# Expert stage of a cross-attention and mixture-of-experts kernel: seven masked tiles, three-wide elementwise operations, no GpSimd work

## The reference, cut to what matters

```python
top_p, top_i = jax.lax.top_k(probs, K)                      # K = 2 of E = 8
for _ in range(NUM_ITER):                                   # 2
    ctx = jnp.concatenate([integrated, v], axis=-1)
    shared_ctrl = _gelu(ctx @ w_s1 + b_s1) @ w_s2 + b_s2
    x_shared, v_shared = _inl(shared_ctrl, integrated, v, mu)
    hidden = _gelu(jnp.einsum('tc,tch->th', ctx_e, w1) + b1)   # w1, b1 of the token's two experts
    ctrl = jnp.einsum('th,tho->to', hidden, w2) + b2
    x_r, v_r = _inl(ctrl, x_e, v_e, mu)
    x_r = (x_r * flat_w).reshape(B * N, K, Dm).sum(axis=1)
    v_r = (v_r * flat_w).reshape(B * N, K, Dm).sum(axis=1)
    x_next = sw * x_shared + (1.0 - sw) * x_r
    v_next = sw * v_shared + (1.0 - sw) * v_r
    halt = jax.nn.sigmoid(_gelu(x_next @ w_h1 + b_h1) @ w_h2 + b_h2)
    refined = _gelu(x_next @ w_f1 + b_f1) @ w_f2 + b_f2
    integrated = integrated + halt * refined * integration_weight
    v = v_next
```

## Time and profile before

| what | us |
|---|---|
| runs (3): median, lowest, highest | 426.99, 422.50, 427.07 |
| profiled execution, first to last instruction (span) | 421.0 |
| PE, DVE, ACT, POOL busy in it | 382.0, 330.7, 203.8, 79.4 |

### The profile page before, as it was taken

One profiled execution on the slowest core, in us unless ns is written; L12 is line 12 of the kernel. 1 busy time (PEld: TensorE's weight loads), 2 busy tenths in 40 slices (PEclk: granted clock), 3 DMA queues, 4 the chain that ended last, 5 costly groups with the idle time before them and its releaser, 6 DMA issues.

```text
span 421.0 us, 4354 instructions
## 1 busy us (share of the span) xinstructions
PE 382.0 (91%) x1394; PEld 220.2 (52%) x1394; DVE 330.7 (79%) x744; ACT 203.8 (48%) x295; POOL 79.4 (19%) x62
## 2 busy tenths in 40 slices
PE   4999997899968799799999899999999999999774
PEld 4746963545635355365545535646464573647521
DVE  0748757655775899897999997997899699799593
ACT  2401135665655725726558256364644635463922
POOL 0210011000010002032231340361015007201500
PEclk9989999999998969889899899999999999979978
DMA  8999320000000000000000000000000000000001
GB/s 275 427 359 303 136 75 1 2 0 0 2 1 0 2 0 1 2 0 1 0 0 2 1 0 0 2 0 0 2 1 0 0 2 26 0 2 1 25 0 51
DMA packets 10727, 17.87 MB, mean 42 GB/s; under 512 B 336, under 2 KB 8528, under 8 KB 9552
## 3 DMA queue, kind: packets, MB, share of 16 engines
q1 hardware_dynamic: 10704, 17.59, 12.1%
HBM read 16.54 MB, written 1.05 MB: 42 GB/s over the span
## 4 chain that ended last, share of the span: by engine, by line
PE 54%; DVE 26%; ACT 8%; issue 7%; POOL 2%; DMA 1%; POOLq 0%; SPq 0%; DVEq 0%; ACTq 0%
PE bank L1010 51%; DVE ring L794 4%; DVE zz L709 3%; DVE hm_lo L803 2%; DVE hm_hi L799 2%; POOL lrs L290 2%; DVE lst L694 2%; DMA ctxT<-in_ctxT 1%; DVE b L968 1%; ACT vtok L534 1%; ACT L534 1%; PE bank L1093 1%; DVE b L976 1%; ACT L483 1%; DVE kT L991 1%
## 5 line engine op out<-in xcount | busy, mean ns | idle before, releaser
L794 DVE SCALAR_TENSOR_TENSOR ring<-ring,pB 128x512 f32<-128x512 f32 x64 | 59.0, 961 | 18.3 <-issue 10.1
L1010 PE MATMUL bank<-hm_hi,ew_hi 128*128 128x512 f32 x160 | 71.6, 447 | 0.0
L1010 PE MATMUL bank<-hm_hi,ew_lo 128*128 128x512 f32 x160 | 64.8, 405 | 0.0
L1010 PE MATMUL bank<-hm_lo,ew_hi 128*128 128x512 f32 x160 | 64.6, 404 | 0.0
L1010 PE MATMUL bank<-xi,pB 128*128 128x512 f32 (+2 forms) x88 | 45.6, 621 | 2.5 <-ACT xi L357 0.7
L803 DVE TENSOR_TENSOR hm_lo<-ring,hm_hi 128x512 fp32r<-128x512 f32 x64 | 41.0, 679 | 0.0
L1010 PEld LDWEIGHTS bank<-hm_hi,ew_hi 128*128 128x128 f32 x160 | 32.3, 202 | 7.4 <-issue 1.3
L1010 PEld LDWEIGHTS bank<-hm_hi,ew_lo 128*128 128x128 f32 x160 | 31.9, 199 | 6.8
L1010 PEld LDWEIGHTS bank<-hm_lo,ew_hi 128*128 128x128 f32 x160 | 31.5, 197 | 7.2
L426 ACT ACTIVATE ring<-bank,pB 128x512 f32<-128x512 f32 x32 | 21.9, 688 | 21.4 <-PE bank L1010 21.4
L290 POOL TENSOR_TENSOR lrs<-lve,mhalf 128x4 f32<-128x4 f32 x12 | 12.1, 1007 | 105.9 <-DVE lve L699 105.9
(11 more groups left out here) (215 smaller groups left out, 667.8 us busy)
## 6 DMA issues: line engine op xcount, KB each, us to landing
ring<-in_fc1b SPq DMA_DIRECT2D x4, 1024.0 KB, 17.3
ring<-in_fc2a SPq DMA_DIRECT2D x4, 1024.0 KB, 9.2
...
a<-in_fc1a SPq DMA_DIRECT2D x1, 1024.0 KB, 13.1
...
```

The source lines that it names most:

```text
L794: dve.scalar_tensor_tensor(hm[j % 2], idxb[:, c, k, :], W("tile_expert", j, j + 1), hid[:, j, :], ALU.is_equal, ALU.mult).then_inc(sem("hm ...
L1010: return pe.matmul(out, lhsT, rhs, start=start, stop=stop)
```

## The change

The expert stage is written anew. The two slots of a token are now sorted by expert number (the smaller first), and the expert tiles are stored in the order 0, 7, 1 to 6. Expert 0 can only be in the first slot and expert 7 only in the second, so that tile 0 serves both slots at once and there are 7 masked tiles. The control networks of shared, first and second slot write three neighbouring banks (`group_ps`), and all activations and most DVE operations take the three streams as one operand of 1536 columns. Tile 0 and its bias are multiplied as halves of 64 rows. The shared hidden units stand twice on the partitions and are cut into fp32r parts as well (`shared_halves`). GpSimd's share goes to DVE. `refine` runs one step later, `bias_parts` moves to slot 1 after the load of one pack `in_C` (1344 KB in place of 768 KB), and `route` and `weigh` are written with compares and reductions over 4 x 8 values, each waiting for the one before (`link`): 15 operations in place of 15, and 8 in place of 5. The index tile is bf16.

The core of the diff (removed lines stand above, apart from those of GpSimd):

```diff
+ORDER = (0, 7, 1, 2, 3, 4, 5, 6)
+TILES = ((0, None), (1, 0), (1, 1), (2, 0), (2, 1), (3, 0), (3, 1))
+NT = len(TILES)
...
+            sp.dma_start(ring[:, PC0:PC0 + nC], d_packC).then_inc(sem("in_C"), 16)
...
-            def refined(s):
-                c = s % NCH
-                pool.wait_ge(sem("rr"), 2 * s + 2)
-                pool.tensor_tensor(xi[:, ck(c)], xi[:, ck(c)], rr, ALU.add).then_inc(sem("xi"), 1)
-                if s >= NCH:
-                    pool.wait_ge(sem("xi"), s + 1)
-                    pool.tensor_tensor(res[:, ck(c)], xi[:, ck(c)], xT[:, ck(c)], ALU.add)\
-                        .then_inc(sem("res"), 1)
-            for s in range(STEPS):
-                c = s % NCH
...
-                for k in range(2):
-                    pool.tensor_tensor(ew[:, 2 + k, :], ew[:, 0, :], cb[:, c, k, :], ALU.mult)\
-                        .then_inc(sem("ew"), 1)
...
+            def squashed(s, part):
+                n = group_of(s, part)
+                act.wait_ge(sem("part_ps"), n + 1)
+                if s >= 1:
                     act.wait_ge(sem("xn"), s)
...
+                if part == BETA:
+                    act.activation(bg[:, 0], group_ps(n), ACT.Abs).then_inc(sem("ab"), 1)
+                    act.wait_ge(sem("ab"), 2 * s + 1)
+                    act.activation(bg[:, 0], bg[:, 0], ACT.Tanh, scale=0.5).then_inc(sem("ab"), 1)
+                    act.wait_ge(sem("ab"), 2 * s + 2)
+                    act.activation(bg[:, 0], bg[:, 0], ACT.Ln, bias=half_col[:, 0:1], scale=0.5)\
+                        .then_inc(sem("squash"), 1)
+                else:
+                    out = al if part == ALPHA else bg[:, 1]
+                    act.activation(out, group_ps(n), ACT.Tanh, scale=0.5).then_inc(sem("squash"), 1)
...
             for s in range(STEPS):
...
                 if s + 1 < STEPS:
                     hidden_gelus(s + 1)
...
+                if s >= 2:
+                    refine2(s - 2)
+                if s < NCH:
+                    squashed(s, GATE)
+                    if s == 0:
+                        expand_evac(NCH - 1, 7, 6)
+                    squashed(s, BETA)
+                    if s >= 1:
+                        refine1(s - 1)
                 else:
...
+                    squashed(s, ALPHA)
+                    squashed(s, GATE)
                     refine1(s - 1)
...
+                    squashed(s, BETA)
+            refine2(STEPS - 2)
             refine1(STEPS - 1)
             refine2(STEPS - 1)
...
+                    bias_parts()
...
+                    hidden_masked(0, (0,))
+                    hidden_masked(0, (1, 2))
                 if q:
                     route(t - 2)
                 if f:
                     ln_scale("att", t)
...
+            hidden_masked(0, (3, 4))
             weigh(NCH - 1)
...
+            hidden_masked(0, (5, 6))
+            shared_halves(0)
+            dve.wait_ge(sem("consts"), 2)
+            def stepped(s):
+                c, it2 = s % NCH, s >= NCH
+                x, v = xi[:, ck(c)], vT[:, ck(c)]
+                def thrice(a):
+                    return a.unsqueeze(1).to_broadcast([128, 3, CH])
+                if it2:
+                    dve.wait_ge(sem("squash"), group_of(s, ALPHA) + 1)
+                    link(dve.scalar_tensor_tensor(al, al, 1.0, thrice(v), ALU.add, ALU.mult))
+                link(dve.tensor_scalar(ne, x, W("mu"), -1.0, ALU.subtract, ALU.mult))
+                dve.wait_ge(sem("squash"), group_of(s, GATE) + 1)
+                dve.wait_ge(sem("squash"), group_of(s, BETA) + 1)
+                dve.scalar_tensor_tensor(bg[:, 0], group_ps(group_of(s, BETA)), 0.0, bg[:, 0],
+                                         ALU.max, ALU.subtract).then_inc(sem("sp"), 1)
...
+                if it2:
+                    link(dve.tensor_tensor(bg[:, 0], bg[:, 0], thrice(ne), ALU.mult))
+                    link(dve.scalar_tensor_tensor(al, al, 0.5, bg[:, 0], ALU.mult, ALU.add))
+                    link(dve.scalar_tensor_tensor(bg[:, 1], bg[:, 1], 1.0, al, ALU.add, ALU.mult))
+                    link(dve.tensor_tensor(bg[:, 1, 1:3], bg[:, 1, 1:3], cb[:, c], ALU.mult))
+                    both = bg[:, 1]
+                    link(dve.scalar_tensor_tensor(both[:, 0], both[:, 0], swc[:, 2:3], both[:, 1],
+                                                  ALU.mult, ALU.add))
+                    link(dve.tensor_tensor(both[:, 0], both[:, 0], both[:, 2], ALU.add))
+                else:
+                    link(dve.tensor_tensor(bg[:, 0, 1:3], bg[:, 0, 1:3], cb[:, c], ALU.mult))
+                    link(dve.scalar_tensor_tensor(bg[:, 1], bg[:, 1], 1.0, bg[:, 0], ALU.add, ALU.mult))
+                    link(dve.scalar_tensor_tensor(bg[:, :, 0], bg[:, :, 0], swc[:, 2:3], bg[:, :, 1],
+                                                  ALU.mult, ALU.add))
+                    link(dve.tensor_tensor(bg[:, :, 0], bg[:, :, 0], bg[:, :, 2], ALU.add))
+                    dve.tensor_tensor(v, bg[:, 0, 0], ne, ALU.mult).then_inc(sem("v1"), 1)
+                    link(dve.tensor_tensor(bg[:, 1, 0], bg[:, 1, 0], ne, ALU.mult))
+                if s >= 1:
+                    dve.wait_ge(sem("h1_ps"), s)
+                dve.scalar_tensor_tensor(xn, bg[:, 1, 0], 0.05, x, ALU.mult, ALU.add).then_inc(sem("xn"), 1)
...
             for s in range(STEPS):
...
                 if s >= 1:
...
+                    stepped(s - 1)
+                if s >= 2:
+                    refine(s - 2)
...
+                    for tiles in ((0,), (1, 2), (3, 4), (5, 6)):
+                        hidden_masked(s + 1, tiles)
+                    shared_halves(s + 1)
+                if s == 0:
+                    slot_masks(NCH - 1)
+                    slot_weights(NCH - 1, 7, 6)
+            stepped(STEPS - 1)
+            refine(STEPS - 2)
             refine(STEPS - 1)
...
+            def controls(s, part):
...
+                n = group_of(s, part)
+                o = slice(part * D, (part + 1) * D)
+                sh, lo, hi = (bank[3 * (n % 2) + k] for k in range(3))
+                top, bot = slice(0, 64), slice(64, 128)
+                m = masked(s)
+                h = hsh[:, s % 2, :]
...
+                if n >= 2:
+                    r, was = owner(n - 2)
+                    if was == BETA:
+                        pe.wait_ge(sem("sp"), r + 1)
+                    else:
+                        pe.wait_ge(sem("squash"), n - 1)
+                pe.wait_ge(sem("m72"), c + 1)
+                pe.wait_ge(sem("hsl"), s + 1)
+                pe.wait_ge(sem("hlo"), NT * s + 1)
+                w_hi, w_lo = weights(ew2_hi, 0), weights(ew2_lo, 0)
+                mm(lo, bp_e[top, o], m72[top, ck(c)], stop=False)
+                mm(hi, bp_e[bot, o], m72[bot, ck(c)], stop=False)
+                mm(lo, w_hi[top, :], m[top, 0, 0, :], start=False, stop=False)
+                mm(hi, w_hi[bot, :], m[bot, 0, 0, :], start=False, stop=False)
+                mm(lo, w_lo[top, :], m[top, 0, 0, :], start=False, stop=False)
+                mm(hi, w_lo[bot, :], m[bot, 0, 0, :], start=False, stop=False)
+                mm(lo, w_hi[top, :], m[top, 1, 0, :], start=False, stop=False)
+                mm(hi, w_hi[bot, :], m[bot, 1, 0, :], start=False, stop=False)
+                mm(sh, ws2_lo[top, o], h[top, :], stop=False)
+                mm(sh, bp_s[top, o], onesb[top, :], start=False, stop=False)
+                mm(sh, ws2_hi[:, o], h, start=False)
+                for i in range(1, NT):
+                    j, k = TILES[i]
+                    pe.wait_ge(sem("hlo"), NT * s + i + 1)
+                    out = hi if k else lo
+                    mm(out, weights(ew2_hi, j), m[:, 0, i, :], start=False, stop=False)
+                    mm(out, weights(ew2_lo, j), m[:, 0, i, :], start=False, stop=False)
+                    last = mm(out, weights(ew2_hi, j), m[:, 1, i, :], start=False, stop=j == HT - 1)
+                last.then_inc(sem("part_ps"), 1)
...
+                pe.wait_ge(sem("h1"), s + 1)
+                if s + 3 < STEPS:
+                    pe.wait_ge(sem("hid"), HT * (s + 4))
+                    pe.wait_ge(sem("hs"), s + 4)
...
                 if s + 1 < STEPS:
                     hidden(s + 1)
...
+                if s >= 2:
+                    refine_b(s - 2)
+                if s < NCH:
+                    controls(s, GATE)
+                    if s == 0:
+                        pe.wait_ge(sem("hid"), 2 * HT)
+                        pe.wait_ge(sem("hs"), 2)
+                        expand(NCH - 1, 7, 6)
+                    controls(s, BETA)
+                    if s == 0:
+                        expand_weights(NCH - 1, 7, 6)
+                    else:
+                        refine_a(s - 1)
+                else:
+                    controls(s, ALPHA)
+                    controls(s, GATE)
                     refine_a(s - 1)
...
+                    controls(s, BETA)
```

(56 more changed lines are left out.)

510 lines of the change are left out of this document (172 added, 338 removed).

## The result

The changed kernel takes **474.0 us** (median of 4 runs, 473.33 to 475.18), the kernel before 424.75 beside it (4 runs): a ratio of **1.1176**, 95% interval 1.1112 to 1.1240. Predicted were 472, range 448 to 494, slower with a chance of 0.88. The profiled execution has a span of 471.5 us.

The account below looks back on a forecast made before the run. PE was taken as the bound, kept fed by interleaved gelus, with a new wait behind beta. First product 173.7, stage 292, clock 12, less 8 for halves: 470 us span, plus 2 gives 472; range 448 to 494.

Parts of the forecast that it names:

- first product of the stage: PE's first expert-stage product, after all seven masked tiles, route, weigh and the shared halves: claimed at 173.7 us.
- step 0: First step of the expert stage, two groups of products and 16 transposes: claimed to take 15.4 us.
- step 1, 2, 3: Early expert-stage steps: 25.4 us without refinement yet, 30.6 with refinement ahead of the gelus, 34.6 with doubled hidden tiles.
- step 4, 5, 6: Expert-stage steps: 44.7 us with a refinement behind beta and doubled hidden tiles, then 40.6 each in iteration 2.
- step 7, tail: End of the expert stage: 30.0 us without hidden tiles, ACT waiting for xn(6); then 30.3 us to the end.
- clock: PE's granted clock after waits in the expert stage: half speed adds 1.7 us, seven times, 12 us; bounds 0 and 22.
- halves: Tile 0's half-height products on PE, perhaps side by side: 8 us saved, the middle of 0 and 17.
- The wait behind beta: After beta's products PE does two hidden tiles, then waits for ACT's abs, tanh, ln, two table loads and gelu: 8.2 us.
- list of what to look for: Expected profile: PE idle once per step behind beta's last product, 5 to 6 us, released by a gelu; clock falling.
- The rival in which PE stays at half speed until the products begin: Low clock after each expert-stage wait lasts longer, 20 to 42 us over all: about 495 to 510 us; chance 0.10.
- The start: Before the expert stage, DVE's bias cutting, route and weigh exposed: 8 + 7 + 2 = 17 us, 12 taken, bounds 4 to 17.
- Queues don't hold PE: Expert stage: beta's ACT work ends before PE's first two hidden tiles, so engines' own sums decide: 415 us; chance 0.06.

Follow-up runs that it names:

- e11: Changed kernel with useless products filling PE's waits where they stand: 24 ahead of wh1 in three refinements, 18 within hidden tiles of four steps; 468.5 us.
- e12: Changed kernel with all eight half products of tile 0 reading the upper 64 rows, so none run on different array halves (wrong values); 494.5 us.
- e4: Changed kernel with the four upper-half products of tile 0 first, then the four lower ones, in place of alternating; 474.3 us.
- e2: Changed kernel without ACT's tanh and ln of beta, leaving only the abs before the hidden gelus; 421.8 us, ratio 0.9955 to the kernel before.
- e7: Changed kernel with beta's group ahead of gate's in each step, on PE and ACT, DVE's list unchanged; 447.6 us.
- e8: e7 plus ACT's tanh of gate moved behind the first gelus, DVE waiting for it only where it reads it; 425.0 us, ratio 1.0013.
- e6: Changed kernel with 24 or 18 useless products between the second and third hidden tile of steps 2 to 7; 487.7 us.
- e9: e8 plus the 16 bias operations cut up and spread over places in slots 1 to 3 where DVE waited for PE; 417.3 us.

## Why the prediction held, step by step

| term | predicted | measured | where |
|---|---|---|---|
| first masked tile | 156.7 | 159.96 | DVE, first L778 |
| first product of the stage | 173.7 | 177.3 | PE |
| step 0 | 15.4 | 14.5 | first product to abs |
| step 1, 2, 3 | 25.4, 30.6, 34.6 | 25.8, 31.6, 35.3 | starts of abs |
| step 4, 5, 6 | 44.7, 40.6, 40.6 | 45.4, 40.4, 40.8 | same |
| step 7, tail | 30.0, 30.3 | 28.7, 31.7 | same |
| clock | +12 | about +12, of which 9.9 seen | e11 |
| halves | -8 | about -11 | e12, e4 |

The predicted steps hold neither clock nor halves; the measured ones hold both, which nearly cancel, as they did in the sum (+12 - 8). From the first product on, 296 us were predicted and 294.2 measured; the first product came 3.6 us late. So the mechanism was right, but that 472 and 474.0 lie 2 us apart is in part luck: a start too early by 3.6 and halves too dear by 3 cancel, and the clock's sum holds seven waits of 1.7 where there were six of about 2.1.

- **The wait behind beta** was priced at 8.2 us from beta's products to the gelu and took 8.1. e2 shows that it hangs on ACT's stretch, e7 and e8 that its place decides. In steps 2 to 4 the wait stands ahead of wh1 and not of a hidden tile; the prediction had `refine1` there, but its list of what to look for spoke of the hidden gelus alone, and e6 was misplaced because I followed the list.
- **The clock** was right in sum: 1.7 us a wait was foreseen, 1.4 to 2.6 came out, behind six waits (4.1 us in step 1, 6.2 in steps 2 to 4, 4.5 in steps 5 and 6) and not seven. The rival in which PE stays at half speed until the products begin did not come: it is back at 0.86 from 342.14, and the products of step 5 begin at 348.69.
- **The halves** were the term without a row. The overlap is whole (0.92 us a group), not half. The change of shape seems to cost about 0.3: between 349.61 and the first products of whole height the starts are further apart than 0.23. Net 6.09 in place of 6.7, 11 us over 18 groups. The rule of the Trainium skill on parallel tiles (TensorEngine Tiling (Array Packing), Key Properties) holds here: different tiles multiply at the same time. The same section says that a change of tiling mode drains TensorE; if that drain is those 0.3 us, it is small, and no run shows it apart.
- **The start** was the worst term: 12 taken, 15.2 measured, within the bounds of 4 and 17. The biases cost their full 8.0, and `route` 2.9 us (105.91 to 108.79) as priced; I had granted the slots too much cover for the rest. The larger load cost nothing, as taken: from 71.15 to 82.63 DVE waits for no DMA. e9 shows that there is cover for 5.5 us, but only for work that stands at the waits.
- **The other rivals.** "Queues don't hold PE", 415 us, is what e2 (421.8) and e8 (425.0) turn the kernel into. Its engine sums were right in steps 2, 5 and 6 (24.0, 33.9 and 33.7 in e2), too high in step 1 (19.0 for 24.8), and too low in steps 3 and 4 (28.0 and 37.0 for 24.8 and 33.9); its condition was not met. That DVE's work lies beside PE's held: DVE is busy for 27.2 of the 40.4 us of step 5, and its 56 masked operations take 746 ns each on the mean, near half of the pair's 1.40 without GpSimd.
